# Attention with keys on partitions: scores on top of a negated row maximum, no turns of the probabilities

## What is computed

```python
q, k = _rope(_layernorm(q, ...)), _rope(_layernorm(k, ...))
k, v = jnp.repeat(k, 4, axis=1), jnp.repeat(v, 4, axis=1)
scores = jnp.einsum('bhqd,bhkd->bhqk', q, k) / math.sqrt(D)
scores = jnp.where(causal[None, None], scores, -jnp.inf)
attn = jax.nn.softmax(scores, axis=-1)
out = jnp.einsum('bhqk,bhkd->bhqd', attn, v)
out = out * jax.nn.sigmoid(gate)
return out @ w_o.T
```

## Time and profile before

| | |
|---|---|
| median of three runs | 1535.22 us |
| span of the profiled execution | 1534.4 us |
| PE busy | 1501.5 us (98%) |
| VectorE (DVE) busy | 1304.1 us (85%) |
| ScalarE (ACT) busy | 1152.4 us (75%) |
| GpSimd (POOL) busy | 364.7 us (24%) |
| DMA, mean | 51 GB/s |

### The profile page before, as it was taken

How to read it: one execution, slowest core, us unless ns; L and a number is a source line. 1 busy time by engine, 2 the same in 40 slices (tenths; PEclk the granted TensorE clock), 3 DMA queues, 4 the chain that set the end, 5 groups by cost and what they waited for, 6 DMA issues and landing times.

```text
span 1534.4 us, 29715 instructions
## 1 busy us (share of the span) xinstructions
PE 1501.5 (98%) x10589; PEld 1380.6 (90%) x10589; DVE 1304.1 (85%) x3037; ACT 1152.4 (75%) x3017; POOL 364.7 (24%) x502
## 2 busy tenths in 40 slices
PE   5999999999999999999999999999999999999998
PEld 3889999999989999999998999999999899999998
DVE  8999888888998888788799888877879888887788
ACT  4777776778887778777878777777787877768765
POOL 6545434420322111111042211111104221011010
PEclk8999999999999999999999999999999999999999
DMA  5411011011121111111111110111022211001013
GB/s 175 163 38 46 28 43 51 30 53 49 60 60 49 35 42 49 39 39 39 59 59 59 40 49 12 49 39 39 20 74 63 60 49 42 18 22 31 9 50 124
DMA packets 45124, 78.82 MB, mean 51 GB/s; under 512 B 4784, under 2 KB 30896, under 8 KB 44784
## 3 DMA queue, kind: packets, MB, share of 16 engines
q1 hardware_dynamic: 41232, 66.65, 14.2%
q0 software_dynamic: 3744, 10.26, 1.9%
HBM read 58.25 MB, written 24.72 MB: 54 GB/s over the span
## 4 chain that ended last, share of the span: by engine, by line
PE 86%; DVE 8%; ACT 3%; issue 2%; DMA 1%; POOL 1%; SPq 0%; DVEq 0%; ACTq 0%; POOLq 0%
PE bank L1392 45%; PE o_bank L1392 22%; PE pt_bank L1467 14%; PE bank L1445 2%; PE bank L1488 2%; DVE t_same L1266 1%; DVE pT_lo L1316 1%; ACT probs L1017 1%; DVE bank L1299 1%; DVE t_same L1262 1%; ACT pT_hi L1036 1%; DVE neg_chunk_max L1302 1%; DVE sumsq L1234 1%; DVE t_same L1250 1%; PE bank L1509 1%
## 5 line engine op out<-in xcount | busy, mean ns | idle before, releaser
L1017 ACT ACTIVATE probs<-bank,neg_max 128x512 f32<-128x512 f32 (+3 forms) x640 | 400.0, 635 | 100.8 <-DVE neg_max L1309 61.5
L1316 DVE TENSOR_TENSOR pT_lo<-pt_bank,pT_hi 128x512 fp32r<-128x512 f32 (+1 forms) x576 | 369.5, 655 | 87.4 <-ACT pT_hi L1036 82.9
L1036 ACT ACTIVATE pT_hi<-pt_bank 128x512 fp32r<-128x512 f32 (+1 forms) x576 | 326.7, 579 | 119.7 <-PE o_bank L1392 59.3
L1392 PE MATMUL o_bank<-pT_hi,v_hi 128*128 128x256 f32 x1088 | 331.8, 305 | 0.4 <-DVE pT_lo L1316 0.3
L1467 PE MATMUL pt_bank<-ident_rows,probs 128*128 128x128 f32 x2176 | 313.3, 273 | 2.5 <-DVE pT_lo L1316 1.5
L1392 PE MATMUL o_bank<-pT_hi,v_lo 128*128 128x256 f32 x1088 | 307.2, 282 | 0.0
L1392 PE MATMUL o_bank<-pT_lo,v_hi 128*128 128x256 f32 x1088 | 306.6, 282 | 0.0
L1302 DVE TENSOR_REDUCE neg_chunk_max<-bank 128x1 f32<-128x512 f32 (+1 forms) x384 | 244.8, 651 | 58.7 <-PE bank L1392 58.1
L1467 PEld LDWEIGHTS pt_bank<-ident_rows,probs 128*128 128x128 f32 x2176 | 252.1, 140 | 25.2 <-DVE pT_lo L1316 3.8
L1392 PE MATMUL bank<-kT_hi,qT_hi 128*128 128x512 f32 (+3 forms) x640 | 242.7, 379 | 0.7 <-ACT probs L1017 0.6
L1392 PE MATMUL bank<-kT_hi,qT_lo 128*128 128x512 f32 (+3 forms) x640 | 231.2, 361 | 0.0
(11 more groups left out here) (167 smaller groups left out, 2852.1 us busy)
## 6 DMA issues: line engine op xcount, KB each, us to landing
norm_rows<-kept_tables SPq DMA_DIRECT2D x24, 384.0 KB, 3.1
made_tables<-kept_tables SPq DMA_DIRECT2D x24, 384.0 KB, 3.0
kept_tables<-made_tables SPq DMA_DIRECT2D x16, 384.0 KB, 2.5
rows<-xs SPq DMA_DIRECT2D x23, 258.0 KB, 2.7
expert_raw<-in_w_fc SPq DMA_DIRECT2D x23, 256.0 KB, 3.0
expert_raw<-in_w_proj SPq DMA_DIRECT2D x23, 256.0 KB, 2.7
xs<-in_x_fill SPq DMA_DIRECT2D x11, 516.0 KB, 5.4
w_raw<-in_w_in SPq DMA_DIRECT2D x7, 640.0 KB, 4.2
```

The lines of the kernel that those rows point to most:

```text
L1017: act.activation(probs[:, u, h % 2, first:first + width], bank("scores", g, t, h, c)[:, 0:width], ACT.Exp, bias=neg_max[:, u, h % 2:h % 2 ...
L1036: act.activation(pT_hi[:, n % PT_RING, 0:width], pt_bank[n % 2][:, 0:width], ACT.Copy)\
L1316: dve.tensor_tensor(pT_lo[:, n % PT_RING, 0:width], pt_bank[n % 2][:, 0:width], pT_hi[:, n % PT_RING, 0:width].bitcast(F32), ALU.subtract) ...
L1392: ins = pe.matmul(out_ap, s, m, start=(start and done == 1), stop=(stop and done == last))
```

## The change

Per query tile the kernel now works in two stages.

1. **Row minimum from one pass.** `A` (L1515) multiplies only the high parts of q and k, queries on partitions, over all keys of the tile. DVE takes the minimum of each chunk straight from PSUM (the bank is then free), and `min` over the chunks. The 512 numbers (4 heads by 128 queries) are stored to DRAM (`mu_store`, elements of 4 bytes), loaded back spread over all 128 partitions (`mu_load`, 256 KB), and for the diagonal block POOL adds the causal mask (`masked`).
2. **Scores with keys on partitions.** For each block j of 128 keys, all four heads at once (512 columns): ACT copies the negated minima into one of three PSUM banks (`seed`), PE adds the three passes of K*Q on top without clearing (`st`), ACT takes exp into `pT_raw` in SBUF (ring of three), again ACT the high part, DVE the low part, now SBUF minus SBUF, and PE multiplies with V, 512 columns wide. There are 544 such tiles. Probabilities need no turn.

The row sum lies across partitions now: POOL adds the P tiles up into `lane_sum` (`psum`, 484 operations of 128x512), PE turns that once per query tile (`SUMT`), DVE reduces and inverts (`sums`). The inverse again goes over DRAM to all partitions (`inv_store`, `inv_load`). The gate is projected directly with channels on partitions, for four query tiles at a time (`G`), DVE multiplies it with `o_bank` (`og0`, takes the place of ACT's copy), and POOL multiplies with the inverse (`og`). The tables BEGIN and DUE are new and shorter; four shared banks instead of five, with no rule which of them scores may use. Of BEGIN and DUE a line stands below.

```diff
-NBANK = 5
+NBANK = 4
+ST_BANKS = 3
+RAW_RING = 3
 PT_RING = 3
...
-DUE = {"table": 42.61, "qkv": -42.78, "rope": -12.87, "turn": -307.03, "v_lo": -73.08, "gate": 9.23,
...
+DUE = {"table": 11.27, "qkv": -2, "rope": -6.98, "rope_lead": 22.27, "turn": 5, "v_lo": 2, "gate": 9.38,
...
+            add("sp mu", ("mu_store", g, t), 0.45, [mu], last - 20, 2)
+            add("sp mu", ("mu_load", g, t), 0.45, [("mu_store", g, t), old(t2, "seed", t2[1]) if t2 else None], last - 20, 256)
+            add("pool mask", ("masked", g, t), 1.27, [("mu_load", g, t), old(t1, "seed", t1[1]) if t1 else None],
+                b + (after - b) * t / (t + 1) + DUE["masked"])
...
+                elif kind == "psum":
...
+                    w.wait_ge(exp_done, m + 1)
...
+                        w.wait_ge(summed, number[step] - 1)
+                        pool.tensor_tensor(total, pT_raw[:, (m - 1) % RAW_RING] if j == 1 else total, pT_raw[:, m % RAW_RING],
+                                           ALU.add).then_inc(summed, 1)
+                elif kind == "og":
...
+                    pool.tensor_tensor(oT[:, t % 2], oT[:, t % 2], inv_rows[:, t % 2], ALU.mult).then_inc(og_done, 1)
...
+                elif kind == "seed":
...
+                        w.wait_ge(exp_done, m - ST_BANKS + 1)
+                    if j == t:
+                        w.wait_ge(masked_done, n + 1)
+                    else:
+                        w.wait_ge(min_back[t % 2], 16 * (n // 2 + 1))
+                    act.activation(st_bank[m % ST_BANKS][:], masked_min[:] if j == t else min_rows[:, t % 2], ACT.Copy, scale=-1.0)\
+                        .then_inc(seeded, 1)
...
+                    w.wait_ge(st_filled, m + 1)
+                    if m >= RAW_RING:
+
+                        w.wait_ge(pt_lo_done, m - RAW_RING + 1)
+                        w.wait_ge(summed, raw_freed(m - RAW_RING))
+                    act.activation(pT_raw[:, m % RAW_RING], st_bank[m % ST_BANKS][:], ACT.Exp, scale=-1.0).then_inc(exp_done, 1)
...
+                    dve.tensor_tensor(pT_lo[:, m % PT_RING], pT_raw[:, m % RAW_RING], pT_hi[:, m % PT_RING].bitcast(F32),
+                                      ALU.subtract).then_inc(pt_lo_done, 1)
...
+                elif kind == "A":
...
+                    pe.matmul(bank("A", g, t, h, c)[:, 0:width], qT_hi[:, t % 2, heads], kT_hi[:, keys], start=True, stop=True)\
+                        .then_inc(filled, 1)
+                elif kind == "st":
...
+                    w.wait_ge(seeded, m + 1)
+                    three(st_bank[m % ST_BANKS][:], [(kT_hi[:, keys], kT_lo[:, keys])], [(qT_hi[:, t % 2], qT_lo[:, t % 2])],
+                          start=False, seeded_bank=True).then_inc(st_filled, 1)
...
+                    three(o_bank[:], [(v_hi[:, j, :], v_lo[:, j, :])], [(pT_hi[:, m % PT_RING], pT_lo[:, m % PT_RING])],
+                          start=(j == 0), stop=(j == t)).then_inc(pv_done, 1)
```

More of the change, by code:

```diff
@@ L395, in plan_program @@
     held = [None] * NBANK
-    width = ["any"]
     place = dict.fromkeys(queues, 0)
@@ L399, in plan_program @@
     transfers = 0.0
-    def banks_for(step):
-        if step[0] == "scores":
-            return SCORE_BANKS[len(chunks_of(step[2]))]
-        return OTHER_BANKS[width[0]]
     def bank_for(step):
         free = []
-        for b in banks_for(step):
+        for b in range(NBANK):
             if held[b] is None:
@@ L462, in plan_program @@
             bank_of[step], prior[step], held[b] = b, held[b], step
-            if step[0] == "scores":
-                g, t, h, c = step[1:]
-                last_scores = t == T - 1 and h == HG - 1 and c == len(chunks_of(t)) - 1
-                width[0] = "any" if last_scores else len(chunks_of(t))
         clock[engine] = start + cost[step]
@@ L713, in tile_before, with raw_freed @@
             return (g, t - n) if t >= n else (g - 1, T + t - n)
+        tile_number = {tile: m for m, tile in enumerate(score_tiles())}
+        def raw_freed(m):
+            g, t, j = score_tiles()[m]
+            return number["psum", g, t, 1 if t and not j else j]
         block = ctx.enter_context(nc.Block())
```

563 lines of the change are left out of this document (300 added, 263 removed), and 27 rows, old and new, of the table BEGIN.

## The result

| | time, us | ratio to before (95% interval) |
|---|---|---|
| before, on the same chip | 1534.8 (1534.33 to 1535.95) | |
| changed | 2369.56 (2363.69 to 2377.11, 4 runs) | 1.5441 (1.5411 to 1.5472) |

A forecast was written before the change was run, and what follows sets the result against it. VectorE (DVE) was to be the bound, held up by GpSimd: 1330 us of work + 307 of waiting + 13 for the ends + 27 of idling = 1677 us. That case's range was 1540 to 1800, chance 0.66; overall range 1500 to 1800.

The forecast's parts named there:

- PE's sum: TensorE's work: turns, wider P*V and the new one-pass product net 124 us less, so PE alone would allow 1410.
- ACT's bound of 1273: ScalarE's work: seed, exp and high part for 544 tiles, at most 1152 + 121 = 1273 us, not the bound.
- POOL's 1120 of work: GpSimd: 611 new 512-wide operations of 1.24 us, 758 us; busy some 1120 in all, on its own below the others.
- The exclusion: DVE operations with two SBUF inputs and wide POOL operations exclude each other, the later waiting; 307 us of new DVE waiting.
- the forecast's terms: VectorE: about 1330 us of its own work plus 307 us waiting for GpSimd.
- its formula: VectorE's waiting: 1218 two-SBUF-input operations x POOL's share of time 0.56 x mean wait 0.45 us = 307 us.
- The idle time of the engine that is the bound: DVE's idling: 13 us for the two ends plus 2%, 27 us, for now and then lacking something.
- rival 3: Both at once, rings of three too short for a DVE held up in bursts; DVE idle 8% more, 1830 us; chance 0.10.
- rival 2: Row maximum's way over DRAM becomes the limit: 7.1 to 10.9 us per trip, 1510 us with PE otherwise bound; chance 0.10.
- the 11.6: Length in us of the row maximum's path over DRAM above which the kernel would be slower than today, PE otherwise bound.
- SP's queue: Row maximum's store and load stand behind expert loads waiting for GpSimd or DVE; said to add to the path, no size.
- The signs: In the changed profile: PE and ACT waiting for min_rows and the load from DRAM while DVE idles.

The follow-up runs named there:

- The run with everything on PE: Changed kernel, row maximum kept, with both DRAM trips replaced by PE turns and ACT copies, and row sums moved from GpSimd to PE; 1716.25 us, ratio 1.1186.

## Why the prediction was wrong, step by step

**PE, ACT, POOL.** PE's sum was close: of the 1410 that PE alone would allow, 1501.5 - 124 = 1377 is busy time. The run with everything on PE has 1612 busy at a clock of 0.993; less 141 for the sums and 55 for the trips that is 1416, 3% more. ACT's bound of 1273 held (1238). POOL's 1120 of work became 1259; its 420 longer additions (1.39 for 1.24) are 65 of that.

**The exclusion** was the right mechanism, mis-sized. For the kernel without trips the forecast's terms are 1330 + 307 = 1637 of VectorE busy; measured 1683, 46 more. For the 420 additions alone its formula gives 1218 x (420 x 1.24 / 1675) x 0.50 = 189 us; measured 254. It let an operation start at any moment and wait for one GpSimd operation; the trace has waits for two in a row. That `pT_lo` came out at 0.922 where 0.93 was expected is luck: with the 2362 us of this run the formula gives 0.68 + 941 / 2362 x 0.45 = 0.86, and for the kernel without trips 0.91, where 0.98 was measured.

The idle time of the engine that is the bound was the worse term: 40 us forecast, 152 measured, about the 8% of rival 3, whose 1830 is nearly the 1837 of this run. That rival's cause, rings of three, was not tested on this kernel; without the one-pass product rings of four gained nothing, and with the sums on PE rings of three let PE be 97% busy. What makes VectorE idle here I have not isolated: its longest waits are 49 us for the one-pass product's banks and 31 for `pT_hi`, and PE's turns of q and k wait 156 us for the rotation.

**The step that failed is the price of rival 2's store.** It was bounded by plain transfers, 2.1 to 5.9 us, with the remark that no row had 4-byte pieces, and then the sum was made as if 5.9 were an end. It took 7.9 to 12.7 us, median 8.9, and with nothing else running still 8.1. The load behind it, put at 3, took 4.6. With the 2 us for reductions, seed and handovers the path is 15.5 us, beyond the 11.6 at which the same paragraph says that the rival decides; its 7.1 to 10.9 lay wholly on the other side. By the paragraph's own sum 15.5 - 9.7 = 5.8 us more in each of 64 tiles is 371 us; this trip alone cost 266. An operation that no row shows, 512 pieces for 2 KB, had to have an open upper end, and rival 2 a chance well over 0.10.

Three further things were missing. The second trip, for the inverse sums, was in no sum, though its store has the same form; it costs 213 us alone. The two together cost 532, and 1677 + 160 + 532 is the 2369 measured. SP's queue was named ("adds to it") and not priced; it stood 1024 us on the two stores. And "when DVE is the bound its gap is stretched and part of it is hidden" did not come about: the planner packs the order for a 2 us landing, and 298 us came back from the order alone. What a chain through DRAM costs was also counted at PE's full clock; behind the gap of 5.87 us shown above a pass took 0.42 us for 0.23.

Two slips in its arithmetic change nothing: 1534 - 1330 - 13 - 27 is 164 and not 161, and the sum with waits that are not 0.13 shorter comes to about 1745 and not 1735.

**The signs** named for this rival came true word for word: PE and ACT waiting for `min_rows` and the load while DVE idles.

## What to carry to other kernels

A round trip through DRAM to turn 512 numbers from partitions to the free dimension costs 13 to 14 us here (8.9 and 4.6 in the median); with 16-byte pieces it has 1.8 for the store and 3.8 for the load; done on chip with four transposes and a copy, 127 of them cost 36 us more than leaving them out. Before giving an idle engine work, ask what it reads: 420 additions on a GpSimd that was three quarters empty cost VectorE, the coming bound, 254 us, 0.6 each. And a planner's landing constant is part of the change: when a new kind of transfer comes in, its measured landing has to go in with it.

## What the runs showed that I had not expected

- 512 pieces of 4 bytes land after 8.1 us with nothing else running, 128 of 16 bytes after 1.4, for the same 2 KB.
- VectorE operations with two SBUF inputs issued without a gap kept a GpSimd addition and a GpSimd copy waiting for 24 us each and were themselves not slowed (0.60 us each). The other way round a VectorE operation waited for two GpSimd operations in a row (2.87 us for 0.68).
- The same 420 additions make a `pT_lo` cost 0.92 us in 2362 us, 0.98 in 1835 and 1.02 in 1684. It is not the length alone: without the inverse's trip it costs 1.00 in 2156. So a cost per operation does not carry over from one order to another.
